# Second layer of a two-layer kernel: gating product one scan behind its block, residual's addition four turns later, picks' places in PSUM

## The chip, the cores and the metric

The kernel runs on one core of one Trainium2 chip. The time is that of one launch on the device, in microseconds (us). The kernel before takes 4823.72 us (median of three runs, 4823.07 to 4824.93).

## The reference, cut to what matters

Two layers run over 8192 tokens (four sequences of 2048) of width 256: `x + attention(norm(x))`, then `x + experts(norm(x))`, twice. The change touches the second layer alone: a selective scan (the "attention" of that layer), and the routing of the experts behind it.

```python
x_ssm, res = jnp.split(x @ W_in.T, 2, axis=-1)          # 512 channels each
x_ssm = silu(causal_conv4(x_ssm) + b_conv)
dt = softplus(x_ssm @ W_dt.T + b_dt)
# 16 states per channel: one recurrence over time for each of 512 x 16 pairs
h = exp(dt * A) * h + dt * B * x_ssm
y = h.sum(over states) + D * x_ssm
y = (y * silu(res)) @ W_out.T
x = x + y                                                # the residual
# two groups of 32 experts, the 2 best of each for every token
logits = norm(x) @ router_w;  expert_weights, expert_indices = top_k(softmax(logits), 2)
order = argsort(expert_indices)                          # every pick gets a row, sorted by expert
```

## The kernel before, in words

Engines: TensorE (PE), VectorE (DVE), ScalarE (ACT), GpSimd (POOL) and SyncE (SP, which issues most DMAs). Each has one queue of instructions and takes them strictly in the order in which the Python code emits them. Semaphores tie them together: `mark` counts an instruction, `after` makes the next instruction of an engine wait for marks.

The second layer works on 16 chunks of 512 tokens. The function `scans` is a loop over 64 recurrences ("scans") for each chunk: 4 blocks of 128 channels (`e`), with 16 states in each (`n`). In this text the scans of a chunk are numbered 0 to 63, so that block 0 ends with scan 15, block 1 with scan 31. In turn `g` of the loop are emitted, in this order:

- POOL: `dbx`, the input of two scans (L1528, every other turn); ACT: the decay exp(dt*A) of scan g into PSUM (L1535), which may be three scans ahead (`ND`).
- DVE: scan g-2 (L1546), into one of eight buffers `hs` (`NR`).
- DVE, after the last scan of a block: the gating product (L1553), which multiplies the finished sum of the block in PSUM bank 7 (`YB`) with silu(res), in turn g = last scan + 4. It waits for PE's sum of the block's last scan. One bank holds the sums of all blocks, so PE can't begin the next block's sum (L1567, the skip term; wait on `"y free"`) before this product has ended.
- PE: the sum over states, scan g-3: four 128x128 transposes that add into the bank (L1571). I call these four matmuls "a sum".
- `background.pull()`: pieces of other stages, at a fixed rate for each. The stage `after_scan` (rate 1.2 pieces a turn) takes the chunk before: four groups of transposes of the gated product (L1071), four of the product with `W_out` (L207, in two banks), a pause of `LAG + 2` pieces, the residual's addition (L1309, which waits for the product), norm statistics (L1036, L1040), the norm on ACT, transposes, the router, and the places of the picks (L1386 to L1394). The stage `main` (rate 0.8) prepares the chunk ahead: products with `W_in` (L207), a convolution by four matmuls with diagonal taps (L1164), silu on ACT with a table load on either side (L1173, L1174). `sizes` makes dt (L1232 to L1257). POOL scatters sorted rows by indirect DMAs (L1475).

These stages share four banks of PSUM (`G`). A stage that finds all four taken gives its turn back, so a bank that is held longer moves the other stages' instructions. The profile counts each fp32 matmul of the program twice where the moving side is 128x256 or 128x512 (two `W_in` matmuls are x4 in a row of the trace), and so for L1567; sums and transposes are counted once.

## Time and profile before

| | |
|---|---|
| median of three runs | 4823.72 us |
| profiled execution, its own time | 4822.83 us |
| its span, first to last instruction | 4821.0 us |
| first scan begins, last scan begins | 2502.5 us, 4142.5 us |
| scans that start in the second layer | 1024 (16 chunks of 64) |
| busy over the span | PE 89%, DVE 77%, POOL 62%, ACT 52% |
| busy in the scans' 200 us from 3200 us | PE 180.1, DVE 179.7, POOL 175.3, ACT 155.9 us |

Rows of the trace give the start (us from the span's first instruction), the time taken, the engine, the source line, the operation, what it writes and reads, and how many equal instructions the row merges. Brackets hold the idle time of that engine just ahead, and what ended it. An engine's instructions overlap a little: a scan of 1.25 us starts every 1.18 us.

### The profile page before, as it was taken

The numbers are of one execution on the slowest core, as the hardware profiler recorded it, in microseconds if no ns is written. First come the engines' busy times: TensorE is split into PE (matmuls) and PEld (weight loads), VectorE is DVE, ScalarE is ACT, GpSimd is POOL, SyncE is SP. The second block draws the span as 40 slices with busy tenths as digits, with TensorE's granted clock in tenths as the row PEclk, the third lists the DMA queues.
The fourth block names the chain that finished last, engine by engine and source line by source line (L and its number), as shares of the span: only waits on it lengthen the run. The fifth ranks groups of instructions, "written<-read, shape, count | busy, mean of one in ns | idle before, by whom it ended". The sixth has DMA issues, their size and how long they took to land. (4 is left out here: it accounts for less than half of the span.)

```text
span 4821.0 us, 59211 instructions
## 1 busy us (share of the span) xinstructions
PE 4269.6 (89%) x19350; PEld 2845.4 (59%) x19350; DVE 3709.2 (77%) x5917; ACT 2521.4 (52%) x4939; POOL 3002.8 (62%) x1908
## 2 busy tenths in 40 slices
PE   5689999999999999998989988989989988599993
PEld 1345566555566555565656566666556666488883
DVE  6887777787778787776128999988999989555677
ACT  1343334344334344333458777777877777255552
POOL 3445545465545455554147888888888889655552
PEclk7899999999999999999999999999999999699997
DMA  4233323333333333332121122121122122596887
GB/s 145 83 105 105 110 88 104 107 104 107 108 96 97 110 99 112 105 102 85 54 85 49 67 78 99 71 74 67 71 82 99 69 69 71 180 254 196 266 278 279
DMA packets 304193, 545.54 MB, mean 113 GB/s; under 512 B 31504, under 2 KB 148496, under 8 KB 294928
## 3 DMA queue, kind: packets, MB, share of 16 engines
q1 hardware_dynamic: 275664, 465.56, 30.0%
q0 software_dynamic: 27648, 75.67, 4.4%
q8 instruction: 157, 2.57, 0.2%
q14 instruction: 148, 1.21, 0.1%
q10 hardware_dynamic: 576, 0.53, 0.1%
HBM read 422.72 MB, written 118.92 MB: 112 GB/s over the span
## 5 line engine op out<-in xcount | busy, mean ns | idle before, releaser
L1528 POOL TENSOR_TENSOR c_dbx<-c_dtx,c_Brep 128x1024 f32<-128x1024 f32 x512 | 1203.0, 2363 | 159.2 <-DVE c_hs L1546 119.0
L876 POOL TENSOR_TENSOR a_kv<-a_rk,a_kv 128x512 f32<-128x512 f32 x512 | 807.3, 1589 | 404.4 <-DMA a_kv<-v_rows 404.2
L1546 DVE TENSOR_TENSOR_SCAN c_hs<-psum,c_carry,c_dbx 128x512 f32<-128x512 f32 x768 | 934.6, 1263 | 56.3 <-ACT psum L1535 41.7
L885 DVE TENSOR_TENSOR_SCAN a_S<-a_decay,a_carry,a_kv 128x513 f32<-128x513 f32 x512 | 792.6, 1548 | 181.6 <-POOL a_kv L876 93.3
L802 POOL TENSOR_TENSOR a_hid_e<-a_hid_e,a_g_rep 128x512 f32<-128x512 f32 x256 | 387.1, 1514 | 772.7 <-ACT a_hid_e L791 590.4
L1535 ACT ACTIVATE psum<-c_dt,c_cols 128x512 f32<-128x512 f32 x1024 | 695.2, 688 | 285.6 <-DVE c_hs L1546 283.6
L1571 PEld LDWEIGHTS psum<-ident,c_hs 128*128 128x128 f32 x4096 | 491.9, 145 | 343.2 <-DVE c_hs L1546 169.7
L1571 PE MATMUL psum<-ident,c_hs 128*128 128x128 f32 x4096 | 596.6, 282 | 87.3 <-DVE c_hs L1546 85.1
L891 DVE TENSOR_TENSOR a_prod<-a_rk,a_S 128x512 f32<-128x512 f32 x512 | 546.4, 1067 | 71.9 <-PE psum L907 71.8
L783 PE MATMUL psum<-a_W_down,a_hid_e 128*128 128x256 f32 x2304 | 550.8, 385 | 54.0 <-POOL a_hid_e L802 29.7
L207 PE MATMUL psum<-a_xT,a_W_up 128*128 128x512 f32 x1152 | 559.5, 616 | 14.7 <-ACT a_hid_e L791 14.6
L783 PEld LDWEIGHTS psum<-a_W_down,a_hid_e 128*128 128x128 f32 x2304 | 436.1, 192 | 219.3 <-issue 83.2
L1934 POOL DMA_INDIRECT results<-d_ys,d_to_row x320 | 312.1, 975 | 231.7 <-issue 154.4
L207 PEld LDWEIGHTS psum<-a_xT,a_W_up 128*128 128x128 f32 x1152 | 217.6, 194 | 253.3 <-issue 209.5
L791 ACT ACTIVATE a_hid_e<-psum 128x512 f32<-128x512 f32 x288 | 171.2, 595 | 339.6 <-PE psum L207 338.7
L2025 PE MATMUL psum<-d_w,d_xT 128*128 x1280 | 332.1, 382 | 0.9 <-issue 0.9
L1546 DVE TENSOR_TENSOR_SCAN c_hs<-psum,c_dbx 128x512 f32<-128x512 f32 x256 | 296.7, 1204 | 34.5 <-ACT psum L1535 18.3
L1475 POOL DMA_INDIRECT sorted_rows<-route_xn,route_to_row x240 | 245.5, 1023 | 84.1 <-issue 38.4
L1232 PE MATMUL psum<-c_xs,c_W_dt 128*128 128x512 f32 x512 | 269.5, 609 | 11.2 <-ACT c_gate L1195 11.2
L207 PE MATMUL psum<-a_xT,a_w 128*128 128x256 f32 x1024 | 239.9, 382 | 12.0 <-ACT a_decay L475 8.9
L658 PE MATMUL psum<-a_w,a_hid_f 128*128 128x256 f32 x1024 | 244.5, 382 | 6.0 <-DVE a_xb L674 3.4
L1164 PE MATMUL psum<-c_pre,c_taps 128*128 128x512 f32 x512 | 242.5, 596 | 0.0
(287 smaller groups left out, 6817.4 us busy)
## 6 DMA issues: line engine op xcount, KB each, us to landing
a_kv<-v_rows SPq DMA_DIRECT2D x512, 256.0 KB
a_g_rep<-g_rows SPq DMA_DIRECT2D x256, 256.0 KB, 3.9
c_Brep<-b_rows SPq DMA_DIRECT2D x64, 1024.0 KB, 6.0
d_xs<-sorted_rows SPq DMA_DIRECT2D x320, 128.5 KB
d_w<-results SPq DMA_DIRECT2D x64, 512.0 KB, 11.4
d_w<-in_d_experts SPq DMA_DIRECT2D x32, 768.0 KB
a_xa<-in_L_attn_x SPq DMA_DIRECT2D x16, 512.0 KB, 4.7
v_rows<-a_rv SPq DMA_DIRECT2D x16, 512.0 KB, 3.0
```

The costliest lines, as they stand in the source:

```text
L207: last = nc.tensor.matmul(out, lhsT, rhs, start=(n == 0), stop=(n == len(pairs) - 1))
L783: m_down = nc.tensor.matmul(banks[t // 2][1][:, (t % 2) * D:(t % 2 + 1) * D], hid_e[:, r, t * P:(t + 1) * P], W_down[:, q, :], start=(q == ...
L802: hid[e - 1] = m_done["gate used", n] = pool.mark(nc.gpsimd.tensor_tensor(hid_e[:, r, :], hid_e[:, r, :], g_rep[:, n % NG, :], ALU.mult))
L876: m_kv[g] = pool.mark(nc.gpsimd.tensor_tensor(kv[:, g % NV, 1:C + 1], rk[slot][:, 1, hb, :], kv[:, g % NV, 1:C + 1], ALU.mult))
L885: m_scan[q] = dve.mark(nc.vector.tensor_tensor_scan(S[:, q % NS, :], decay[cq % 2][:, hb, :], kv[:, q % NV, :], carry[:, sq_:sq_ + 1], ALU ...
L891: m_prod[q] = dve.mark(nc.vector.tensor_tensor(prod[:, q % NP, :], rk[cq % 2][:, 0, sq_ // DK, :], S[:, q % NS, 0:C], ALU.mult))
L1528: m_dbx[g] = m_dbx[g + 1] = pool.mark(nc.gpsimd.tensor_tensor(dbx[:, r:r + 2, :], dtx[slot][:, e, :].unsqueeze(1).broadcast_to([P, 2, C]), ...
L1535: m_da[g] = act.mark(nc.scalar.activation(psum[:, DA + g % ND, :], dt[slot][:, e, :], ACT.Exp, scale=A[:, e, n:n + 1]))
L1546: m_scan[q] = dve.mark(nc.vector.tensor_tensor_scan(hs[:, q % NR, :], psum[:, DA + q % ND, :], dbx[:, q % NX, :], first, ALU.mult, ALU.add))
L1571: last = nc.tensor.matmul(psum[:, YB, t * P:(t + 1) * P], hs[:, q % NR, t * P:(t + 1) * P], ident[:, :], is_transpose=True, start=False, s ...
L1934: nc.gpsimd.indirect_dma_start(out=results[j // NT], in_=ys[:, j % NY, :], in_offset=None, out_offset=bass.IndirectOffsetOnAxis(ap=to_row[ ...
L2025: m = nc.tensor.matmul(bank[:, 0:2 * P], xT[:, q % N3, kb * P:(kb + 1) * P], w[:, bass.ds(at_w[q] + kb * 2 * P, 2 * P)], start=(kb == 0), ...
```

## The change

Three edits, all in the second layer.

1. In `scans` the gating product is emitted behind PE's sum in turn g = last scan + 3, not ahead of it in turn g = last scan + 4.
2. The pause between the product with `W_out` and the residual's addition is `LAG + 6` pieces of the stage, not `LAG + 2`.
3. The places of the picks are reduced into the same PSUM bank as the ranks, not into an SBUF tile `place`; the bank is freed by the CAST that reads them, not by the product two instructions earlier.

```diff
-                yield from pause(LAG + 2)
+                yield from pause(LAG + 6)
...
-            ranks = bank[:, 0:TL * NE]
+            ranks, in_room = bank[:, 0:TL * NE], bank[:, TL * NE:TL * NE + TL * Z.picks]
...
-            m = G.freed[i] = dve.mark(nc.vector.tensor_tensor(
+            m = dve.mark(nc.vector.tensor_tensor(
                 at_pick[:, :, :, :], R["onehot"][:, :, :, :],
                 ranks.rearrange("p (r e) -> p r e", e=EX).unsqueeze(2).broadcast_to([P, TL * GR, TOP, EX]), ALU.mult))
...
-            m = dve.mark(nc.vector.tensor_reduce(flat(place[:, :, :, :].rearrange("p t g k -> p t (g k)")), at_pick[:, :, :, :].rearrange("p r s e -> p (r s) e"), AX, ALU.add))
+            m = dve.mark(nc.vector.tensor_reduce(in_room, at_pick[:, :, :, :].rearrange("p r s e -> p (r s) e"), AX, ALU.add))
...
-            m_done["placed", c] = [dve.mark(nc.vector.tensor_copy(flat(route.to_row[:, c % 2, :, :]), flat(place[:, :, :, :].rearrange("p t g k -> p t (g k)")))), m_xn]
+            m = G.freed[i] = dve.mark(nc.vector.tensor_copy(flat(route.to_row[:, c % 2, :, :]), in_room))
+            m_done["placed", c] = [m, m_xn]
...
-                q = g - AHEAD - 2
-                if 0 <= q < total and q % N == N - 1:
-                    cq, sq = divmod(q, steps)
-                    e = sq // N
-                    background.drain(until=lambda: is_done(("gate", cq)))
-                    dve.after(m_sum[q], m_done["gate", cq])
-                    m_done["gated", cq, e] = m_done["y free"] = dve.mark(nc.vector.tensor_tensor(
-                        gate[cq % 2][:, :, e * P:(e + 1) * P], psum[:, YB, :].rearrange("p (t d) -> p t d", t=TL),
-                        gate[cq % 2][:, :, e * P:(e + 1) * P], ALU.mult))
                 q = g - AHEAD - 1
...
                     if sq == steps - 1:
                         m_done["scanned", cq] = [m_dbx[q], m_da[q], m_sum[q]]
+                q = g - AHEAD - 1
+                if 0 <= q < total and q % N == N - 1:
+                    cq, sq = divmod(q, steps)
+                    e = sq // N
+                    background.drain(until=lambda: is_done(("gate", cq)))
+                    dve.after(m_sum[q], m_done["gate", cq])
+                    m_done["gated", cq, e] = m_done["y free"] = dve.mark(nc.vector.tensor_tensor(
+                        gate[cq % 2][:, :, e * P:(e + 1) * P], psum[:, YB, :].rearrange("p (t d) -> p t d", t=TL),
+                        gate[cq % 2][:, :, e * P:(e + 1) * P], ALU.mult))
```

The order of the program moves with it. Below, the eighth chunk (c = 7), whose pattern is that of chunks 1 to 14. Scans are named `SCALAR_TENSOR_TENSOR c_hs`.

DVE before, from behind scan 1 of the chunk to scan 17 and its neighbours (the L1553 rows are the gating products of the chunk before and of block 0):

```order
L1553 TENSOR_TENSOR c_gate<-psum,c_gate 128x4x128
L1254 TENSOR_TENSOR c_dtx<-psum,c_xs 128x512
L1546 SCALAR_TENSOR_TENSOR c_hs<-psum,c_carry,c_dbx 128x512 x14
L1309 TENSOR_TENSOR c_xb<-c_xb,psum 128x512 x2
L1546 SCALAR_TENSOR_TENSOR c_hs<-psum,c_carry,c_dbx 128x512
L1036 BN_STATS c_stats<-c_xb 128x6 x4
L1040 BN_AGGR c_mv<-c_stats 128x2 x4
L1546 SCALAR_TENSOR_TENSOR c_hs<-psum,c_carry,c_dbx 128x512
L1553 TENSOR_TENSOR c_gate<-psum,c_gate 128x4x128
```

The same stretch of DVE now (the gating product is L1574, scans are L1547):

```order
L1574 TENSOR_TENSOR c_gate<-psum,c_gate 128x4x128
L1250 SCALAR_TENSOR_TENSOR psum<-psum,c_tmp 128x512
L1547 SCALAR_TENSOR_TENSOR c_hs<-psum,c_carry,c_dbx 128x512
L1254 TENSOR_TENSOR c_dtx<-psum,c_xs 128x512
L1547 SCALAR_TENSOR_TENSOR c_hs<-psum,c_carry,c_dbx 128x512 x15
L1574 TENSOR_TENSOR c_gate<-psum,c_gate 128x4x128
L1309 TENSOR_TENSOR c_xb<-c_xb,psum 128x512 x2
L1547 SCALAR_TENSOR_TENSOR c_hs<-psum,c_carry,c_dbx 128x512
L1036 BN_STATS c_stats<-c_xb 128x6 x4
L1040 BN_AGGR c_mv<-c_stats 128x2 x4
```

Before, the addition stood behind scan 15 and the gating product of block 0 behind scan 17. Now the gating product stands behind scan 16, and the addition right behind it.

PE before, from the product with `W_out` to the sums of block 1 (each x4 of L1571 is one sum; the first L1567 row begins block 1):

```order
L1571 MATMUL psum<-ident,c_hs 128x128 x4
L207 MATMUL psum<-c_W_out,c_yT 128x256 x4
L1164 MATMUL psum<-c_pre,c_taps 128x512 x2
L1571 MATMUL psum<-ident,c_hs 128x128 x4
L207 MATMUL psum<-c_W_out,c_yT 128x256 x4
L1571 MATMUL psum<-ident,c_hs 128x128 x20
L207 MATMUL psum<-c_xT,c_W_in 128x512 x2
L1567 MATMUL psum<-c_skip_diag,c_xs 128x128 x4
L1571 MATMUL psum<-ident,c_hs 128x128 x4
L207 MATMUL psum<-c_xT,c_W_in 128x512 x2
L1571 MATMUL psum<-ident,c_hs 128x128 x20
L1164 MATMUL psum<-c_pre,c_taps 128x512 x2
```

PE now, from the last product with `W_out` (the sums are L1563, the skip term L1559):

```order
L207 MATMUL psum<-c_W_out,c_yT 128x256 x8
L1563 MATMUL psum<-ident,c_hs 128x128 x4
L1164 MATMUL psum<-c_pre,c_taps 128x512 x2
...
L1164 MATMUL psum<-c_pre,c_taps 128x512 x2
L1563 MATMUL psum<-ident,c_hs 128x128 x16
L1559 MATMUL psum<-c_skip_diag,c_xs 128x128 x4
L1563 MATMUL psum<-ident,c_hs 128x128 x12
L207 MATMUL psum<-c_xT,c_W_in 128x512 x2
L1563 MATMUL psum<-ident,c_hs 128x128 x4
L207 MATMUL psum<-c_xT,c_W_in 128x512 x2
L1563 MATMUL psum<-ident,c_hs 128x128 x20
L1164 MATMUL psum<-c_pre,c_taps 128x512 x2
```

The same pieces stand ahead of the sum of scan 15 as before, with the products ahead of the taps instead of among them. The two pairs of `W_in` that stood on either side of block 1's beginning now both come three and four sums into block 1. The first transposes of the gated product now stand ahead of the pair of `W_in` at the chunk's beginning, which before stood ahead of the wait for the gating product:

```order
L1563 MATMUL psum<-ident,c_hs 128x128 x24
L1071 MATMUL psum<-ident,c_gate 128x128 x4
L207 MATMUL psum<-c_xT,c_W_in 128x512 x2
L1559 MATMUL psum<-c_skip_diag,c_xs 128x128 x4
L1563 MATMUL psum<-ident,c_hs 128x128 x4
```

On ACT the silu of the second pair of blocks (L1173, with its two table loads) moves from turn 34 to turn 37 of a chunk.

## Rows read from the trace of the kernel before

**Rows 1.** Busy time of the engines in stretches: us, PE, PEld, DVE, ACT, POOL, clock, DMA.
```profile
3200.00:3400.00 200.00, 180.12 (x981) 121.36 (x979) 179.66 (x253) 155.86 (x282) 175.28 (x96) 0.98 0.20 71
...
3110.00:3112.00 2.00, 2.00 (x6) 0.96 (x4) 2.00 (x3) 1.69 (x4) 2.00 (x1) 0.50 0.00 0
```

**Rows 2.** Groups of DVE's instructions, 2510 to 4150 us: busy us, mean ns | idle before.
```profile
L1309 DVE TENSOR_TENSOR c_xb<-c_xb,psum 128x512 f32<-128x512 f32 x31 | 20.8, 675 | 68.5 <-PE psum L207 64.5 <-PE psum L1442 4.0
...
L1394 DVE CAST route_to_row<-c_place 128x16 int32<-128x16 f32 x15 | 11.1, 743 | 0.0
```

**Rows 3.** The line of the CAST, L1394: ns min/median/max.
```profile
L1394 DVE CAST route_to_row<-c_place x16: 139/199/2676, 2677.5 to 4185.6; 128x16 int32<-128x16 f32 x16
```

**Rows 4.** Timeline around one CAST, DVE and POOL.
```profile
3298.98 2.68 DVE L1394 CAST route_to_row<-c_place 128x16 int32<-128x16 f32 x1
3299.25 2.36 POOL L1528 TENSOR_TENSOR c_dbx<-c_dtx,c_Brep 128x1024 f32<-128x1024 f32 x1
```

**Rows 5.** The line of the gating product, L1553: DVE's idle before it; who waited.
```profile
  PE psum L1571: 0.8, 1
...
  PEld psum L1567: 116.6, 62
```

**Rows 6.** Timeline of DVE, chunk 7, scan 0 to the gating product of block 0.
```profile
3212.93 1.25 DVE L1546 TENSOR_TENSOR_SCAN c_hs<-psum,c_carry,c_dbx 128x512 f32<-128x512 f32 x1
...
3215.88 0.66 DVE L1553 TENSOR_TENSOR c_gate<-psum,c_gate 128x512 f32<-128x512 f32 x1
...
3217.06 11.84 DVE L1546 TENSOR_TENSOR_SCAN c_hs<-psum,c_carry,c_dbx 128x512 f32<-128x512 f32 x10
...
3235.24 0.66 DVE L1309 TENSOR_TENSOR c_xb<-c_xb,psum 128x512 f32<-128x512 f32 x1
3239.85 0.69 DVE L1309 TENSOR_TENSOR c_xb<-c_xb,psum 128x512 f32<-128x512 f32 x1 [3.95 <-PE psum L207]
3240.45 1.28 DVE L1546 TENSOR_TENSOR_SCAN c_hs<-psum,c_carry,c_dbx 128x512 f32<-128x512 f32 x1
3241.65 1.38 DVE L1036 BATCH_NORM_STATS2 c_stats<-c_xb 128x6 f32<-128x256 f32 x4
...
3243.47 1.25 DVE L1546 TENSOR_TENSOR_SCAN c_hs<-psum,c_carry,c_dbx 128x512 f32<-128x512 f32 x1
3244.64 0.66 DVE L1553 TENSOR_TENSOR c_gate<-psum,c_gate 128x512 f32<-128x512 f32 x1
```

**Rows 7.** Timeline of PE, the same stretch.
```profile
3213.56 1.88 PE L207 MATMUL psum<-c_xT,c_W_in 128*128 128x512 f32 x4
3216.60 1.16 PE L1567 MATMUL psum<-c_skip_diag,c_xs 128*128 128x128 f32 x8 [1.16 <-DVE c_gate L1553]
...
3235.77 1.88 PE L1164 MATMUL psum<-c_pre,c_taps 128*128 128x512 f32 x4
...
3237.92 1.89 PE L207 MATMUL psum<-c_W_out,c_yT 128*128 128x256 f32 x8
3239.65 2.35 PE L1571 MATMUL psum<-ident,c_hs 128*128 128x128 f32 x20
3241.83 1.88 PE L207 MATMUL psum<-c_xT,c_W_in 128*128 128x512 f32 x4
3245.36 1.16 PE L1567 MATMUL psum<-c_skip_diag,c_xs 128*128 128x128 f32 x8 [1.64 <-DVE c_gate L1553]
```

**Rows 8.** Timeline of DVE, the end of block 1 of that chunk.
```profile
3265.59 0.67 DVE L1553 TENSOR_TENSOR c_gate<-psum,c_gate 128x512 f32<-128x512 f32 x1
3268.03 1.28 DVE L1546 TENSOR_TENSOR_SCAN c_hs<-psum,c_carry,c_dbx 128x512 f32<-128x512 f32 x1 [1.78 <-ACT psum L1535]
```

**Rows 9.** Timeline of PE, the last two sums of that block.
```profile
3263.67 1.04 PE L1571 MATMUL psum<-ident,c_hs 128*128 128x128 f32 x8
```

**Rows 10.** Timeline of ACT, the silu of the second pair of blocks.
```profile
3263.24 1.28 ACT L1173 ACT_TABLE_LOAD   x1
...
3265.82 1.28 ACT L1174 ACT_TABLE_LOAD   x1
3267.12 0.30 ACT L1469 ACTIVATE route_xn<-route_xn,route_ones 128x4 f32<-128x4 f32 x1
```

More of the change, by code:

```diff
@@ L1601, in layer1_phase @@
         at_pick = sb("at_pick", [P, TL * GR, TOP, EX])
-        place, over = sb("place", [P, TL, GR, TOP]), sb("over", [P, NE])
+        over = sb("over", [P, NE])
         R = router_buffers(nc, st, "c", GR, EX, TOP)
```

## The prediction

> **What bounds the kernel now.** I read the busy time by stretches first. In the scans both PE and DVE are busy nine tenths of the time [rows 1], so shares alone name no bound; the question is who waits for whom at which scan. The groups of DVE's instructions come next: the largest wait of one small group is the residual's addition, 64.5 us in all for PE's product with W_out [rows 2], 14 waits, one in each of chunks 1 to 14. The line of the gating product shows the opposite: DVE has waited for PE only once there, 0.8 us, while PE's weight loads wait 116.6 us for the product [rows 5]. Both edits aim at these numbers. Last I read the timelines of DVE and PE side by side in chunk 7, where the clock was at its high level.
>
> What the reader is to see there: scan 15 ends at 3235.3, the addition begins, and its second half waits until 3239.85 [rows 6]. PE at that time is not slow at one product; it is seven us behind as a whole. From the skip term at 3216.60 to the sum of scan 15 it runs without a gap: five sums stand in one row behind the product, to 3242.0 [rows 7]. So the first quarter of a chunk is bound by PE: 25.4 us of matmuls against some 20 us of scans (16 at 1.18 us, from the row of ten [rows 6]). The rest of the chunk is mostly bound by DVE's own work.
>
> **Part 1, the addition and the gating product of block 0.** These two have one answer, since they now stand next to each other. The gating product needs the sum of scan 15, which is the last thing that PE does of its backlog, behind both products that the addition needs. When does that sum end now? The chunk's first gating product (block 3 of the chunk before) needs a sum behind which PE began the pair of W_in at 3213.56 [rows 7], before scan 0 ended, so it starts behind scan 0: 3212.93 + 1.18 = 3214.1 in place of 3215.88, 1.78 us earlier [rows 6]. But in front of it PE had the pair of W_in (from 3213.56, 1.88 us [rows 7]) as cover, and that pair now stands behind the first transposes, which wait for the product. PE starts at 3214.8 and has 25.4 + 1.7 us to do (the pair takes 1.72 until the next can start): 3241.9, against 3242.0 before. The early start is eaten by the lost cover; the rest is the same set of matmuls in another order. So the gating product starts at 3242.0 to 3242.1.
>
> DVE then: scan 16 now runs ahead of it (3235.2 to 3236.5), and DVE waits for 5.6 us, not 3.95. Behind the gating product come the two additions, scan 17, the statistics, and scan 18. By rows 6 the steps from start to start are 0.6 (product), 0.6 and 0.6 (additions), 1.2 (scan), 1.82 (statistics, 3241.65 to 3243.47): scan 18 starts at 3242.05 + 4.8 = 3246.9. Before, it started 0.58 us behind the product at 3244.64, so at 3245.2. DVE is 1.6 us later. The wait of the addition has not gone; it is the gating product's, and what DVE used to do between the end of W_out's product and the end of the sums (scan 16, statistics, scan 17) now stands behind them.
>
> **Part 2, block 1.** PE gets the bank 2.6 us earlier (3242.8 instead of 3245.36 [rows 7]) and would be glad of it, but has nothing to do: both pairs of W_in that stood here now come three and four sums later, and scans 17 and 18 end at 3245.1 and 3248.1. Before, PE went from 3245.36 to the end of sum 31 (3264.7 [rows 9]) in 19.35 us without a gap. Now it has one more pair of W_in in that stretch, 1.72, and I count 4.4 us of idle: 0.9 ahead of sum 17, 2.3 ahead of sum 18, and 1.1 ahead of sums 23 and 24, since the taps come at sum 25 and not at 22. 3242.8 + 19.35 + 1.72 + 4.4 = 3268.3, and the gating product of block 1 starts at 3268.4, not 3265.59 [rows 8]. It has scan 32 ahead of it but no longer scan 33. Scan 34 starts at 3268.4 + 0.6 + 1.2 = 3270.2; before at 3268.03, where it had waited 1.78 us for ACT [rows 8]. DVE is 2.2 us later (the 1.6 of part 1 are in it).
>
> ACT's block of silu and two table loads takes 3263.24 to 3267.12, 3.9 us [rows 10], and it caused that 1.78. It moves from turn 34 to turn 37, so the wait is not gone but comes again behind the gating product's. ACT is at most three scans ahead; with two small router instructions of DVE as cover I get a wait of 1.0 us at scan 37, and take 0.6 of it as new (bounds 0 and 1.78). Sum for a chunk: 2.8 us. Bounds: 1.6, if block 1 loses nothing of its own, and 4.5, if ACT's wait returns in full on top with another small one at the later silu. Times 14: +39 us, +22 to +63. In block 2, by the same timeline, PE's sum ends as scan 1 of the next block does, so the new place costs DVE nothing that counts; in block 3 it is early. Chunk 0, where PE still warms up, I put at +1. Chunk 15 has no W_in and no taps: 0.
>
> **Part 3, the places in PSUM.** One CAST of 128x16 took between 139 and 2676 ns [rows 3], 743 in the mean and 11.1 us for 15 [rows 2]. The long one ended within 0.05 us of POOL's product (3298.98 + 2.68 against 3299.25 + 2.36 [rows 4]): DVE stood still for the whole of POOL's instruction. With its input in PSUM I expect it to take 0.14 to 0.2 us, as the short ones do: (0.743 - 0.17) x 15 = -8.6 us, in block 3, where DVE is the bound. Bounds: -8.6 and 0 (it is held as before). I take -8. The bank is held two instructions longer, which moves some matmuls of W_dt by nothing and others by two sums, hidden in block 3, where PE waits.
>
> The Trainium skill explains this row ("SBUF — State Buffer", section "SBUF: two separate sides"): VectorE and GpSimd share a port pair as an exclusive lock, which a VectorE instruction takes in a two-port mode. By that rule the copy from PSUM needs no lock and the whole 8.6 goes; if the rule didn't hold for this CAST, the time would be 8 us more. The trace agrees with the lock, with its 2.68 us; that PSUM avoids it no run here shows yet.
>
> **Sum.** +39 + 1 - 8 = +32 us on the profiled execution's 4822.8 (its span is 4821.0), and the median of the runs lies 0.9 above that: 4855 us.
>
> **Rivals.** *A: the waits go, as the numbers of the profile suggest.* The addition's 64.5 us vanish and the 8 of the CAST too: 4823 - 64 - 8 = 4751; if half of it comes back elsewhere, 4783. For it: four more turns (3.3 scans, some 4 us) are just the mean wait, 64.5 / 14 = 4.6. Against it: DVE can't pass the gating product, and the sum that this needs ends at 3242, 2.2 us behind the product with W_out [rows 7]. It needs PE to finish the sum of scan 15 four us earlier than I reckon. The Trainium skill ("Perfetto Trace Analysis", section "Optimization Strategy") tells one to find the gaps of the busiest engine and make what they wait for come sooner; followed on the addition's row alone that gives this rival.
>
> *B: nothing to be told from no change* (within 0.2%, about 9.6 us, which is what a measurement of this kernel can tell). PE's 2.6 us earlier skip term carries through block 1, its idle time is filled, and DVE loses the 1.6 of part 1 alone: +22 - 8 - 5 = +9 or less, 4824 to 4832. For it: PE waits for the gating product in 62 of 64 blocks [rows 5]. Against: in the timeline PE has nothing to do at that place.
>
> *C: the loss is larger through PE's clock.* At 3110 to 3112 PE ran at 0.50 of its clock, its lower level of 1.2 GHz, and in these 2 us issued only 6 matmuls [rows 1]; this followed a stretch in which it had waited for scans. New idle of 4.4 us at the head of block 1, which is PE's critical stretch, may bring such a spell there: 3.4 us at half speed cost 1.7 in each of 14 chunks, with part 2's upper bound: 4823 + 63 + 24 - 8 = 4902. It decides only if idle comes in one piece, and mine comes in three.
>
> **How the numbers follow.** My forecast 0.66, its own range 4838 to 4878 (part 2's bounds and part 3's). A 0.12, B 0.14, C 0.08. The range 4808 to 4890 leaves out most of A and half of C. Faster by over 0.2%: A and a sliver of B, 0.14. Same: most of B and the low end of mine, 0.15. Slower: 0.71.
>
> **What would show it.** Right: L1309 no longer waits, and the gating product's line has some 14 waits for PE of 5 to 6 us (block 0) and 14 more of 1 to 3 us (block 1), over 85 us in all; PE's wait at the skip term falls from 116.6 [rows 5] to under 60, with new idle ahead of sums 17 and 18; the chunks' period grows by 2 to 4 us; the CAST's mean falls to below 200 ns. Wrong: if in block 0 the gating product waits for under 3 us, part 1 is wrong and A holds; if block 1's gating product doesn't wait, part 2 is; if the CAST still takes over 1 us at times, part 3.

## The result, and the profile after

The changed kernel takes 4900.36 us (median of 5 runs, 4898.63 to 4905.88), the kernel before 4824.93 beside it (5 runs, 4823.07 to 4831.39): ratio 1.0156, 95% interval 1.0142 to 1.0170, or 75 us more. The forecast was 4855, in a range of 4808 to 4890. The direction was right and the size was not. The profiled execution took 4900.36 us, its span 4898.6; its mean clock was 0.942, against 0.950 before. One slow execution, 13130 us in early_2_4 below, is left out of its ratio.

First the groups of DVE's instructions in the scans, 2510 to 4220 us (busy us, mean ns | idle before), which answer to [rows 2, 5]:

```profile
L1574 DVE TENSOR_TENSOR c_gate<-psum,c_gate 128x512 f32<-128x512 f32 x64 | 43.8, 685 | 127.6 <-PE psum L1563 127.0
...
L1309 DVE TENSOR_TENSOR c_xb<-c_xb,psum 128x512 f32<-128x512 f32 x30 | 19.1, 680 | 0.0
L1394 DVE CAST route_to_row<-psum 128x16 int32<-128x16 f32 x15 | 2.2, 148 | 0.0
```

The addition no longer waits (64.5 us before), and the CAST has become short. But the gating product, now L1574, waits 127 us for the sums (L1563), where it had waited 0.8. Its own line tells the other side (which engine sat idle for it: us, times):

```profile
  PE psum L1563: 127.0, 32
...
  PEld psum L1559: 29.1, 29
```

PE's wait at the skip term fell from 116.6 us [rows 5] to 29.1. So the wait changed hands: DVE now stands where PE stood. The timeline of DVE in chunk 7 (start us, us; scan 0 begins at 3245.2), to be laid beside [rows 6]:

```profile
3246.51 0.69 DVE L1574 TENSOR_TENSOR c_gate<-psum,c_gate 128x512 f32<-128x512 f32 x1
...
3255.61 10.68 DVE L1547 TENSOR_TENSOR_SCAN c_hs<-psum,c_carry,c_dbx 128x512 f32<-128x512 f32 x9 [2.50 <-ACT psum L1536]
...
3270.19 1.28 DVE L1547 TENSOR_TENSOR_SCAN c_hs<-psum,c_carry,c_dbx 128x512 f32<-128x512 f32 x1 [1.13 <-ACT c_carry L1555]
3276.87 0.69 DVE L1574 TENSOR_TENSOR c_gate<-psum,c_gate 128x512 f32<-128x512 f32 x1 [5.39 <-PE psum L1563]
3277.47 1.28 DVE L1309 TENSOR_TENSOR c_xb<-c_xb,psum 128x512 f32<-128x512 f32 x2
3278.66 1.28 DVE L1547 TENSOR_TENSOR_SCAN c_hs<-psum,c_carry,c_dbx 128x512 f32<-128x512 f32 x1
3279.86 1.38 DVE L1036 BATCH_NORM_STATS2 c_stats<-c_xb 128x6 f32<-128x256 f32 x4
...
3303.95 0.69 DVE L1574 TENSOR_TENSOR c_gate<-psum,c_gate 128x512 f32<-128x512 f32 x1 [2.71 <-PE psum L1563]
```

Block 0's product waits 5.39 us, and additions, scan 17 and statistics stand behind it, not in front. Block 1's waits 2.71. PE at the same time, beside [rows 7]:

```profile
3240.03 0.66 PE L1563 MATMUL psum<-ident,c_hs 128*128 128x128 f32 x4 [0.87 <-DVE c_hs L1547]
3241.80 0.95 PE L1563 MATMUL psum<-ident,c_hs 128*128 128x128 f32 x4 [1.12 <-DVE c_hs L1547]
3242.98 3.50 PE L1563 MATMUL psum<-ident,c_hs 128*128 128x128 f32 x12 [0.23 <-DVE c_hs L1547]
...
3248.23 3.62 PE L207 MATMUL psum<-c_xT,c_W_in 128*128 128x512 f32 x4
...
3274.92 1.91 PE L1563 MATMUL psum<-ident,c_hs 128*128 128x128 f32 x16
3277.61 1.16 PE L1559 MATMUL psum<-c_skip_diag,c_xs 128*128 128x128 f32 x8 [0.78 <-DVE c_gate L1574]
3278.61 0.60 PE L1563 MATMUL psum<-ident,c_hs 128*128 128x128 f32 x4
3280.00 0.66 PE L1563 MATMUL psum<-ident,c_hs 128*128 128x128 f32 x4 [0.79 <-DVE c_hs L1547]
3282.99 1.12 PE L1563 MATMUL psum<-ident,c_hs 128*128 128x128 f32 x4 [2.33 <-DVE c_hs L1547]
3283.89 3.13 PE L207 MATMUL psum<-c_xT,c_W_in 128*128 128x512 f32 x4
```

Two things are to be seen. Ahead of sums 17 and 18 PE is idle, as forecast. And a pair of W_in, 1.88 us in [rows 7], takes 3.62 us at the head of the chunk and 3.13 us behind that idle time. The windows of two of those stretches show why (us; busy of PE, PEld, DVE, ACT, POOL; granted clock; DMA):

```profile
3242.00:3246.00 4.00, 3.62 (x15) 2.42 (x14) 4.00 (x5) 3.97 (x8) 3.39 (x3) 0.50 0.74 279
3246.00:3249.00 3.00, 2.12 (x8) 1.32 (x7) 2.97 (x5) 1.35 (x4) 1.80 (x1) 0.50 0.00 0
```

The clock is 0.50, the lower level of 1.2 GHz, just where PE's backlog begins. Added up over the scans, PE ran at that level for 133 us before and for some 210 us after. At the heads of the chunks it did so in 7 of 15 before and in 11 of 15 after, in block 1 in 1 of 14 and in 12 of 14. From the first scan's start to the last's it is 1640.0 us before and 1709.0 after, so 69 of the 75 us lie in the scans.

For the comparisons below I took from each trace the start of every scan, subtracted that of its chunk's scan 0, averaged over chunks 2 to 13 and subtracted the same of before. It is the delay (us) that a chunk has gathered by then; at "64" the next chunk begins. Where two kernels have different work of DVE ahead of a scan, the difference there is not lost or gained time; only the last row is free of that. The kernels are explained below.

```
scan  early_12  late_12  gate_only  pause_only   after  keep_all  psum_keep
 18     +0.5     +1.9      +0.3       -2.3       +2.9     +1.6      -0.1
 34     +0.4     +1.2      +0.7       +0.1       +4.4     +2.1      -0.2
 38     +0.4     +1.2      +2.1       -0.5       +5.5     +3.2      -0.2
 48     +0.4     +1.9      +3.7       -0.9       +6.1     +3.8      -0.2
 52     -0.2     +1.2      +5.1       -1.6       +5.4     +3.1      -0.9
 54     -0.2     +0.1      +5.1       +4.5       +4.3     +2.0      -0.9
 64     -0.2     +1.2      +5.1       +4.5       +5.4     +3.1      -0.9
scan   early_4  early_1_4  early_2_4  early_3_4  early_4_keep
 18     -1.3      -0.3       -1.6       -1.2        -2.7
 34     -2.2      -1.7       -0.6       -2.2        -3.6
 38     -2.1      -1.5       +0.7       -2.0        -3.4
 48     -1.0      -0.2       +2.6       -0.8        -2.2
 64     -1.4      -0.4       +2.6       -0.5        -2.3
```

### The profile page after: what moved, and what is told of

The parts are those of the page before. It is cut to its first block and busy times, and to the rows that moved or that the text cites. A ratio compares the mean times of both kernels' runs of the same rounds, so it can differ in the third digit from the quotient of the medians.

```text
span 4898.6 us, 59190 instructions
## 1 busy us (share of the span) xinstructions
PE 4312.5 (88%) x19350; PEld 2860.5 (58%) x19350; DVE 3705.2 (76%) x5917; ACT 2515.2 (51%) x4939; POOL 2998.6 (61%) x1908
## 5 line engine op out<-in xcount | busy, mean ns | idle before, releaser
L1547 DVE TENSOR_TENSOR_SCAN c_hs<-psum,c_carry,c_dbx 128x512 f32<-128x512 f32 x768 | 938.7, 1268 | 65.4 <-ACT psum L1536 52.8
L1563 PEld LDWEIGHTS psum<-ident,c_hs 128*128 128x128 f32 x4096 | 503.0, 147 | 411.0 <-DVE c_hs L1547 217.3
L1563 PE MATMUL psum<-ident,c_hs 128*128 128x128 f32 x4096 | 622.4, 287 | 119.8 <-DVE c_hs L1547 117.2
L1547 DVE TENSOR_TENSOR_SCAN c_hs<-psum,c_dbx 128x512 f32<-128x512 f32 x256 | 297.3, 1208 | 38.4 <-ACT psum L1536 22.9
```

The costliest lines, as they stand in the source:

```text
L1547: m_scan[q] = dve.mark(nc.vector.tensor_tensor_scan(hs[:, q % NR, :], psum[:, DA + q % ND, :], dbx[:, q % NX, :], first, ALU.mult, ALU.add))
L1563: last = nc.tensor.matmul(psum[:, YB, t * P:(t + 1) * P], hs[:, q % NR, t * P:(t + 1) * P], ident[:, :], is_transpose=True, start=False, s ...
```

## Experiments: each edit alone

The kernel before was measured again beside each group of runs, and its medians lie between 4813.85 and 4824.93 us. So ratios are compared, not times. An expectation given as a time is to be read against 4824.9: 4890 us, for instance, is the ratio 1.0135. In the traces, what lies outside the scans varies from 3170 to 3190 us in no order that follows the edits; the starts of the scans are free of it.

**gate_only.** The kernel before with the product's block moved behind the sum, `q = g - AHEAD - 2` becoming `q = g - AHEAD - 1` (the hunks at 1544 and 1573 of the change).

> The kernel before with the first edit alone: the gating product one scan behind its block; the addition's pause and the picks' places as before. Theory 1 (order and clock): this edit alone moves the matmuls of W_in and the taps, so block 1 suffers as in the changed kernel, but the addition now stands behind scan 13, and the product with W_out comes two sums earlier on PE, so L1309 hardly waits (under 10 us in all against 64.5) and the additions, the statistics and their scan are done before the gating product of block 0, which waits only 2 to 4 us. Scan 18 of a chunk starts about 3 us earlier than in the changed kernel. Expected: 4825 to 4850 us, 50 to 75 below the changed kernel. Rival 2 (the gating edit carries the whole loss, the pause nothing): 4890 to 4909.

Measured: 4882.84 us, ratio 1.0144 (1.0128 to 1.0159). My theory missed, and the number is that of rival 2: this edit alone brings nearly the whole loss. And it doesn't arise in blocks 0 and 1, as I had it, but between scans 34 and 50. There, ACT's silu of the gates with its table loads now stands at turn 48, and the product of block 2 right behind it. Scan 48 waits for ACT 28.1 us in 14 chunks, and the product then 27.0 us for PE (DVE, chunk 7):

```profile
3330.22 1.28 DVE L1546 TENSOR_TENSOR_SCAN c_hs<-psum,c_carry,c_dbx 128x512 f32<-128x512 f32 x1 [1.56 <-ACT psum L1535]
3332.38 0.69 DVE L1573 TENSOR_TENSOR c_gate<-psum,c_gate 128x512 f32<-128x512 f32 x1 [0.87 <-PE psum L1562]
```

**pause_only.**

```diff
-                yield from pause(LAG + 2)
+                yield from pause(LAG + 6)
```

> The kernel before with the second edit alone: pause of LAG + 6. Theory 1: the gating product of block 0 (still two scans behind) now stands ahead of the addition and waits some 4 us for PE's sum, in place of the addition's 4.6; W_in keeps its place, so PE loses nothing and gets the bank 1.7 to 2.6 us earlier. Expected 4805 to 4830. Rival 2 (the pause is what hurts): over 4860. Rival 3 (the addition's wait simply goes, 64 us): 4760 to 4775.

Measured: 4877.04 us, ratio 1.0138 (1.0123 to 1.0154). Missed as well; the number is that of rival 2, and it arises in one place. DVE waits for the rank matmuls (PE's rows, then DVE's, chunk 7):

```profile
3324.34 2.08 PE L1567 MATMUL psum<-c_skip_diag,c_xs 128*128 128x128 f32 x8 [3.77 <-DVE c_gate L1553]
...
3333.22 0.70 PE L1354 MATMUL psum<-route_picked,route_ones 128*128 128x256 f32 x2
```

```profile
3333.96 0.70 DVE L1360 TENSOR_REDUCE route_picked<-route_picked 128x64 f32<-128x320 f32 x1 [4.35 <-PE psum L1354]
```

The pause moves everything behind it in its stage. The rank matmuls went from turn 47 to 51, past the skip term of block 3, which waits for the gating product. DVE waited 53.9 us in 13 such places. In the changed kernel they stand at 48, ahead of the skip term, and this wait isn't there. The -1.6 at scan 52 in the table is no lead: the two reductions, the product and the CAST that before stand behind scans 48 to 50 here come behind scans 53 and 54, and up to scan 52 DVE has been idle 0.7 us per chunk more than before.

**psum_only** (the third edit alone: `in_room = bank[:, TL * NE:...]` as output of the reduce and input of the copy, `G.freed` behind the copy).

> The kernel before with the third edit alone: the picks' places in PSUM. No instruction changes its place. Theory: the CAST's mean falls from 743 to about 150 ns and the time by 8 to 9 us: 4815 to 4818. Rival: the gain is taken up by a wait for POOL just behind, since POOL is free only then: 4822 to 4826.

Measured: 4810.47 us, ratio 0.9991 (0.9982 to 1.0000), some 4 us of the 8 to 9 expected. The CAST took 149 to 174 ns, as expected. In the trace this kernel gains 0.8 us per chunk, 11 us in 14 (10 us from the first scan to the last), a little more than the times allow (0 to 9 us).

The single edits give 1.0144, 1.0138 and 0.9991, all three together 1.0156: the losses don't add up, since most of the second edit's is a place that the first clears.

## Experiments: the clock

**keep_busy** is the changed kernel with matmuls of zeros that add nothing to the sum, at sums behind which PE waits for a scan at the end of a chunk:

```diff
                     m_sum[q] = pe.mark(last)
+                    if e == EB - 1 and 10 <= n < N - 1:
+                        for t in range(2):
+                            nc.tensor.matmul(psum[:, YB, t * P:(t + 1) * P], nothing[:, :], ident[:, :], start=False, stop=False, skip_group_check=True)
```

> The changed kernel with two more matmuls of zeros added into the bank of the sums after each of the sums 58 to 62 of a chunk, where PE only waits for scans; they change no value. Theory 1: about 1.3 us of each chunk's loss is PE's lower clock (0.5) at the head of the chunk, behind PE's idle end of block 3. With PE busy there, the sum of scan 15 ends 29.0 to 29.3 us behind scan 0 in all chunks (mean before the change 29.1, changed 30.4), and the time falls by 15 to 25 us: 4875 to 4885. If the clock stays low or the theory is wrong: 4898 to 4905, or more, since the zeros cost PE some time.

Measured: 4868.49 us, ratio 1.0107 (1.0092 to 1.0123), at the favourable end of what the clock theory said (1.0104 to 1.0125 as ratios). By the ratios half a per cent, 24 us, comes back from doing more work; from the first scan to the last the traces have 14 us less.

**keep_all** adds 4, 12, 6 and 5 more behind sums 16, 17, 34 and 38.

> The changed kernel, with matmuls of zeros added into the sums' bank wherever PE waits for scans: 2 after each of sums 58 to 62, and new 4 after sum 16, 12 after sum 17, 6 after sum 34, 5 after sum 38. In the changed kernel PE ran at 0.50 of its clock for 210 us within the scans; with only the first group of these matmuls it was 122 us, the spells at the head of the chunks were gone, those at 34 to 41 us in a chunk stayed, and the ratio to before fell from 1.0156 to 1.0107. Theory (half of the loss is the clock, half the order of the work): the spells in block 1 go too, low clock under 60 us, sum 31 ends 26.5 us after sum 15 and not 27.4, another 0.8 us per chunk come back: ratio 1.006 to 1.010. Rival (the clock in block 1 costs nothing, since DVE and ACT wait there for each other anyway): ratio stays at 1.011. If the added matmuls are themselves in the way: 1.012 or more.

Measured: 4862.87 us, ratio 1.0082 (1.0068 to 1.0096), low clock 36 us in the scans. The theory held: by the ratios the changed kernel's low clock is worth 36 us, from the first scan to the last 29. The head of a chunk (PE, chunk 7), then DVE at the end of block 0:

```profile
3230.79 0.61 PE L1567 MATMUL psum<-ident,c_nothing 128*128 128x128 f32 x4
3231.50 0.66 PE L1563 MATMUL psum<-ident,c_hs 128*128 128x128 f32 x4
3233.35 0.63 PE L1071 MATMUL psum<-ident,c_gate 128*128 128x128 f32 x4 [1.19 <-DVE c_gate L1576]
3233.81 1.88 PE L207 MATMUL psum<-c_xT,c_W_in 128*128 128x512 f32 x4
```

```profile
3260.45 0.69 DVE L1576 TENSOR_TENSOR c_gate<-psum,c_gate 128x512 f32<-128x512 f32 x1 [4.31 <-PE psum L1563]
3261.06 1.28 DVE L1309 TENSOR_TENSOR c_xb<-c_xb,psum 128x512 f32<-128x512 f32 x2
```

The pair of W_in is back at 1.88 us. In this kernel the sum of scan 15 ends 29.05 us after scan 0 starts in the mean, in the changed one 30.37.

**psum_keep** is psum_only with such matmuls (2 behind sums 58 to 62, 3 behind 44 and 45): does the low clock cost anything before the change?

> The kernel before with the places in PSUM (alone it had the ratio 0.9991) and with matmuls of zeros: 2 after each of sums 58 to 62, 3 after sums 44 and 45. Before, PE ran at 0.50 for 133 us within the scans, mostly at scans 48 to 53, where PE waits anyway, and at the head of five chunks. Theory: only the spells at the head of a chunk cost, some 0.5 us per chunk in the mean, so a ratio of 0.997 to 0.999, the best so far. Rival: the low clock costs before as much as after (about 2 us per chunk): 0.993. Rival: the added matmuls cost what they gain: 1.000 or more.

Measured: 4810.84 us against 4824.29 for before, ratio 0.9973 (0.9964 to 0.9983). As expected, little: 0.2% beside psum_only, with low clock down to 75 us, from 133 before and 119 in psum_only.

## Experiments: the join and the order

Moving the products does two things. It moves the places at which DVE must wait for PE (the join). And since `after_scan` begins when block 3's product is emitted, it moves the other work (W_in from turns 1, 16, 17, 32, 34 to 4, 19, 20, 35, 36; silu from 34 and 45 to 37 and 48; the addition from 16 to 14 without the longer pause). These kernels take the places per block, all with the third edit:

```diff
+                if ... q % N == N - 1 and q % steps // N in LATE:    # q = g - AHEAD - 2, ahead of the sum
...
+                if ... q % N == N - 1 and q % steps // N in EARLY:   # q = g - AHEAD - 1, behind the sum
```

**early_12**: blocks 0 and 1 early, `pause(LAG + 2)`.

> The kernel before with the places in PSUM, and only the gating products of blocks 0 and 1 one scan behind instead of two; those of blocks 2 and 3, and the order of all other work (products, taps, silu, addition at turn 16) stand as before. This is the join of DVE and PE moved, without the order. Theory: block 0 costs the 1.6 us of part 1, block 1 up to 1 us more, since PE gets the bank early but finds no scans: 1.6 to 2.6 us in 14 chunks, less 4 for the places: ratio 1.004 to 1.007, the product waits some 5 to 6 us at scan 16. Rival (it is the order of the matmuls that costs, the join is free): ratio 0.999 to 1.001. Rival (all of the loss is the join): 1.012 to 1.016.

Measured: 4821.88 us, ratio 0.9993 (0.9984 to 1.0002), beside 0.9991 for psum_only. In the old order the early joins are free within the noise, as the first rival had it and my theory did not; from the first scan to the last it takes 6 us more than psum_only. DVE, chunk 7:

```profile
3239.09 0.69 DVE L1309 TENSOR_TENSOR c_xb<-c_xb,psum 128x512 f32<-128x512 f32 x1 [3.97 <-PE psum L207]
3239.69 1.28 DVE L1547 TENSOR_TENSOR_SCAN c_hs<-psum,c_carry,c_dbx 128x512 f32<-128x512 f32 x1
3241.27 0.69 DVE L1583 TENSOR_TENSOR c_gate<-psum,c_gate 128x512 f32<-128x512 f32 x1 [0.30 <-PE psum L1572]
```

The addition's wait of 4 us stands in front of the product; PE finishes its backlog under it, and the product finds its sum ready but for 0.30 us.

**late_12**: the changed kernel with blocks 0 and 1 late (2 and 3 early, `pause(LAG + 6)`).

> The changed kernel in all but one thing: the gating products of blocks 0 and 1 stand two scans behind as before; the order of all other work is that of the changed kernel. This is the order without the join. Theory (both cost, and the clock follows from the idle at the head of block 1): ratio 1.004 to 1.009, with fewer spells of low clock at 34 to 41 us of a chunk. Rival (all of the loss is the join): ratio 0.999 to 1.001. Rival (all of it is the order): 1.014 to 1.016.

Measured: 4835.67 us against 4824.29, ratio 1.0024 (1.0015 to 1.0034). That is between the first rival and the theory's range. So taking the two joins back recovers 1.3 of the 1.56%, though alone they cost nothing that can be told.

**early_4**: only block 3 early, `pause(LAG + 2)`.

> The kernel before with the places in PSUM, and only the gating product of block 3 one scan behind: this starts the work behind the scans earlier and so gives the order of the first edit alone (W_in at turns 4, 19, 20, 35, 36 for 1, 16, 17, 32, 34; silu at 37 and 48 for 34 and 45; addition at 14), while the products of blocks 0, 1 and 2 stay two scans behind. The first edit alone had 1.0144, and lost 4.7 us of its 5.1 per chunk between scans 36 and 50. Theory (the loss there needs both, the later silu and the join at the end of block 2): ratio 1.003 to 1.008. Rival (the order alone): 1.012 to 1.015. Rival (the joins alone): 0.998 to 1.001.

Measured: 4794.98 us against 4816.0, ratio 0.9958 (0.9944 to 0.9972). All three theories missed: the new order alone is a gain. PE, then DVE, at the end of block 0 in chunk 7:

```profile
3234.84 1.91 PE L1572 MATMUL psum<-ident,c_hs 128*128 128x128 f32 x16
3237.53 1.16 PE L1568 MATMUL psum<-c_skip_diag,c_xs 128*128 128x128 f32 x8 [0.78 <-DVE c_gate L1554]
3238.53 1.47 PE L1572 MATMUL psum<-ident,c_hs 128*128 128x128 f32 x12
3239.84 1.88 PE L207 MATMUL psum<-c_xT,c_W_in 128*128 128x512 f32 x4
```

```profile
3226.13 1.26 DVE L1309 TENSOR_TENSOR c_xb<-c_xb,psum 128x512 f32<-128x512 f32 x2
...
3236.79 0.69 DVE L1554 TENSOR_TENSOR c_gate<-psum,c_gate 128x512 f32<-128x512 f32 x1 [2.74 <-PE psum L1572]
```

The addition doesn't wait, and the late products of blocks 0 and 1 now wait too (53.1 us in 26 places in all). DVE does scans 16 and 17 before the product, so three sums (x12) follow the skip term without a gap: the idle time of PE ahead of sums 17 and 18 needs the product in front of those scans.

**early_1_4, early_2_4, early_3_4**: block 3 and one other block early: block 0, 1 or 2 (the labels count blocks from 1).

> As the kernel with only block 3's product one scan behind (ratio 0.9958), and block 0's too. By the traces the first edit alone (all four products early, 1.0144) falls back by 1.6 us per chunk at scan 18, by 1.4 more at scan 34, by 1.2 at scan 38 and by 2.0 at scan 50. Theory (each join costs its own piece, block 0's the 1.6 us of part 1): 1.6 x 14 = 22 us over 0.9958: ratio 0.999 to 1.002. Rival (block 0's join pulls the whole loss behind it, since DVE, ACT and PE then stay in step): 1.010 or more. Rival (block 0's is free, as it was in the old order): 0.996.

> As the kernel with only block 3's product one scan behind (0.9958), and block 1's too. Theory (its own piece, 1.4 us at scan 34, and the wait for ACT's silu at scan 37, 1.1 us, since DVE has no scan left to run ahead with): 1.4 to 2.6 us in 14 chunks, ratio 1.000 to 1.004. Rival (free): 0.996. Rival (without block 0's join it costs only the wait at scan 34): 0.999.

> As the kernel with only block 3's product one scan behind (0.9958), and block 2's too. In this order ACT's silu of the gates (with two table loads) stands at turn 48, and DVE waits for it at scan 48, 1.5 us in 14 chunks, with the product of block 2 behind. Theory (the product then waits for PE as well, as in the first edit alone, where it waited 2.4 us): 1 to 2 us in 14 chunks, ratio 0.999 to 1.002. Rival (free: PE is in front there once blocks 0 and 1 have no early join): 0.996.

Measured: 0.9985 (0.9977 to 0.9994), 1.0056 (1.0043 to 1.0069) and 0.9987 (0.9978 to 0.9996). Beside early_4's 0.9958 the early product costs 0.3% in block 0, 1.0% in block 1 and 0.3% in block 2. The first and the third lie just beneath the theory, the second above it. The three sum up to 1.5%, and gate_only (which lacks the third edit) is 1.9% above early_4. So each join costs its own piece in this order; block 1's is dearest. In gate_only the loss seemed to arise behind scan 34 alone because up to there the new order's gain (early_4: -2.2 at scan 34) covers most of what the joins of blocks 0 and 1 cost (gate_only: +0.7). The early products in early_2_4 (which they waited for: us, times; 15 of the 16 are block 1's):

```profile
  PE psum L1572: 45.5, 16
```

By the table early_2_4 is 1.6 us behind early_4 at scan 34, 2.8 at scan 38 (DVE now waits 1.2 us for ACT's silu at scan 37 in each of 14 chunks, and in early_4 not at all), 3.6 at scan 48 and 4.0 at the end.

late_12 and early_3_4 differ in the pause alone: blocks 2 and 3 early in both, `LAG + 6` in the first and `LAG + 2` in the second. Their ratios are 1.0024 and 0.9987, so the second edit costs 0.37% in this order too. I had made no expectation for this pair.

**act_before and act_after**: psum_keep and keep_all with the silu of the second pair of blocks as an identity and its two table loads left out, in chunks 2 to 15.

```diff
-                    ... activation(xs_[:, e, :], bank, ACT.Silu, bias=b_conv[:, e, :]))
-                nc.scalar.preload_act_table_set("natural_log_exp_and_others")
+                    ... activation(xs_[:, e, :], bank, ACT.Identity if e0 and c > 1 else ACT.Silu, bias=b_conv[:, e, :]))
+                if not (e0 and c > 1):
+                    nc.scalar.preload_act_table_set("natural_log_exp_and_others")
```

> The same left out (silu of the second pair and its two table loads in chunks 2 to 15) in the kernel before with the places in PSUM and the matmuls of zeros (ratio 0.9973). There DVE waits for ACT 1.6 us at scan 34 and 1.4 at scan 31. Theory (ACT's block costs before 1.6 per chunk, as much as or more than after, so that ACT explains little of the difference): ratio 0.990 to 0.994. Rival (the wait at scan 34 is cover for PE and nothing is gained): 0.997. If ACT is what the change made worse, this gains clearly less than the same edit does in the changed kernel.

> The changed kernel with all the matmuls of zeros (ratio 1.0082, low clock 36 us), and left out: the silu of the second pair of blocks in chunks 2 to 15 is an identity, without its two table loads (2 x 1.28 us of ACT per chunk). There DVE waited for ACT 15.1 us in 14 at scan 37, 8.8 us at scan 42, 14.0 us at scan 32. Theory (the waits of 1.03 at scan 37 come from this block and count in full, those at scan 42 belong to the gates' silu and stay, the one at scan 32 hides behind PE): 1.0 us per chunk less, 14 us: ratio 1.004 to 1.006. Rival (the wait turns into one for PE): 1.007 to 1.008. Rival (ACT sets the pace of the whole block): 1.003 or less.

Measured: act_before 0.9913 (0.9899 to 0.9926), from 0.9973; act_after 1.0043 (1.0029 to 1.0057), from 1.0082. By the starts of the scans it is 1.9 us per chunk before and 1.2 after, both near what was expected (1.6 and 1.0). The wait for ACT costs in both, and no more after than before.

**pk_p4**: psum_keep with `pause(LAG + 4)`.

> The kernel before with the places in PSUM and the matmuls of zeros (ratio 0.9973), and the pause ahead of the addition two turns longer: the addition stands at turn 18, behind the gating product of block 0, and not at 16; all gating products stay two scans behind. The pause of four turns alone lost 1.4% by one place only: the rank matmuls came behind the skip term of block 3, and DVE waited 4.35 us for them; up to scan 52 that kernel was 1.6 us per chunk ahead of before. Here they stand at turn 48, ahead of the skip term. Theory: the loss is gone and about 1 us per chunk of the gain stays: ratio 0.993 to 0.997. Rival (the addition's wait only moves to the gating product, 5 us at scan 17, and nothing is gained): 0.997 to 0.999. Rival (any shift of the router's chain loses as in the single edit): over 1.005.

Measured: 4832.8 us against 4816.0, ratio 1.0035 (1.0021 to 1.0049): between the rivals, and a loss. The theory rested on a lead of pause_only up to scan 52, which was none, as said there. The gating product waited 66.2 us in 14 places, and DVE waited for ACT 30.1 us in 14 at scan 34 and 16.7 in 10 at scan 39. Why ACT comes late there I have not settled.

**early_4_keep**: early_4 with the matmuls of keep_busy.

> The kernel with only block 3's product one scan behind (0.9958) with matmuls of zeros, 2 after each of sums 58 to 62. In it PE ran at 0.50 for 58 us around the heads of the chunks, and scan 5 came 1.62 us later after scan 0 than before, with a wait for PE of 22.3 us in 14. Theory (the clock at the head costs what it shows there): that wait goes and about 1 us per chunk comes back, the best version: ratio 0.992 to 0.994. Rival (DVE catches up later anyway, the added matmuls gain as little as in the old order, 0.2%): 0.994 to 0.996.

Measured: 4768.11 us against 4813.85, ratio 0.9899 (0.9885 to 0.9914). It is the fastest version, 46 us below before, and by the ratio gains more than expected (0.6% over early_4, 28 us; from the first scan to the last, 15 us). The pair of W_in at the head of chunk 7 takes 1.88 us, in early_4 3.04. DVE is 1.4 us further ahead at scan 18 than in early_4, and 0.9 at scan 64.

## Why the prediction was wrong in size

Two terms of the sum failed. PE's clock stood at nothing in it, and the runs put it at 2.3 us per chunk, some 32 us. And part 2 took 0.6 us for ACT's waits behind scan 34, which are 1.7 us per chunk, some 15 us more. The mechanism of parts 1 and 2, a wait that changes hands, was right.

**Part 1 (block 0) was right without the clock.** It said that the sum of scan 15 ends 29.0 us after scan 0 starts, as before, and DVE is 1.6 us later at scan 18. In keep_all these are 29.05 and +1.6. In the changed kernel they are 30.37 and +2.9: the difference, 1.3 us per chunk, is the low clock at the head, of which the text said nothing for this place. The product waits 5.39 us in chunk 7 (5.6 forecast).

**Part 2 (block 1) was right as far as scan 34 and too small behind it.** It said +2.2 at scan 34; keep_all has +2.1. The product of block 1 waits 38.5 us in 16 blocks (1 to 3 us each forecast). Behind scan 34 I stopped counting, at 2.8 per chunk. Measured without the clock it is keep_all against psum_keep, 3.1 + 0.9 = 4.0 us, within part 2's bounds. The term that was mis-sized is ACT's wait. In keep_all DVE waits for ACT at scan 37 (1.1 us per chunk, 15.1 us in 14) and again at scan 42 (8.8 us in 14), and in psum_keep at neither (chunk 7, scans 37 and 42):

```profile
3294.09 1.28 DVE L1547 TENSOR_TENSOR_SCAN c_hs<-psum,c_carry,c_dbx 128x512 f32<-128x512 f32 x1 [1.03 <-ACT psum L1536]
...
3303.52 1.28 DVE L1547 TENSOR_TENSOR_SCAN c_hs<-psum,c_carry,c_dbx 128x512 f32<-128x512 f32 x1 [0.57 <-ACT psum L1536]
```

The wait at scan 37 was forecast (1.0), but only 0.6 of it was taken as new; the one at scan 42 stood in the upper bound alone, and it stays in act_after (8.8 us), so it isn't the second pair's silu. Nor is ACT what the change made worse as a whole: that silu costs 1.9 us per chunk before and 1.2 after, and without it the two kernels are further apart, 1.9 + 2.8 = 4.7 us per chunk. My reading is that behind an early join DVE has no scan in hand and meets each late partner separately. early_2_4 against early_4 fits it, with its wait at scan 37, but no run isolates it.

**Rival C was the mechanism that was missing, and it had 0.08.** After minus keep_all is 5.4 - 3.1 = 2.3 us per chunk, 32 us, and by the ratios 0.74% or 36 us. C put 1.7 us per chunk on block 1 and said that it decides only if idle comes in one piece. Ahead of the pair of W_in in block 1 it came in pieces of 0.78, 0.79 and 2.33 us in the rows above, and the pair took 3.13 us. More than half of the cost (1.3 of 2.3 us by scan 18) arose at the head of the chunk, where PE waits 0.2 to 1.1 us for each of the last scans before the backlog starts. Before, such spells stood at the head as well, in some chunks; [rows 1] shows one, and its pair of W_in took 3.54 us where [rows 7] has 1.88:

```profile
3109.57 0.74 PE L1571 MATMUL psum<-ident,c_hs 128*128 128x128 f32 x4 [0.52 <-DVE c_hs L1546]
3110.10 3.54 PE L207 MATMUL psum<-c_xT,c_W_in 128*128 128x512 f32 x4
```

I should have asked what more of them would cost.

**Part 3 was right on the CAST, and its time is within what was measured**: 148 ns in the mean; 8 us taken, 4 measured (0 to 9). With its input in PSUM the longest CAST is 174 ns, where it had been 2676 [rows 3]. The Trainium skill ("SBUF — State Buffer", section "SBUF: two separate sides") describes the lock on the ports that VectorE and GpSimd share; the trace agrees with it.

**Rival A** is refuted: the 64.5 us of the addition went, and 127 us stand at the gating product. **Rival B** needed PE's idle time filled, and it was not.

**The sum.** Per chunk +4.0 (the first two edits without the clock) + 2.3 (clock) - 0.9 (places, and what the added matmuls gain before) = +5.4, times 14 = 75 us. These are means of chunks 2 to 13; the periods of chunks 1 to 14 give +5.0, or 70 us, and the agreement with 75 is partly luck. Forecast: 2.8 x 14 + 1 - 8 = 32 (with 4822.8 and the 0.9 that makes 4855.7, put down as 4855).

**What I had not asked.** I took the change as one thing. Its first edit holds a gain (block 3's product early, -0.33% beside psum_only, which starts the work behind the scans sooner) and three losses (blocks 0 to 2). The second edit is a loss by itself: the longer pause cost 1.4% alone, 0.37% in late_12 against early_3_4, and 0.6% in pk_p4 against psum_keep. In pause_only and pk_p4 the addition no longer waits, and the time still grows. In late_12 PE ran at 0.50 for 123 us at the heads of the chunks, in early_3_4 for 91, which may be part of its cost; the rest stays open.

## What to carry to other kernels

A wait of a busy engine is worth taking away only if the engine it waits for isn't behind as a whole: ask when that engine's backlog ends, and what else joins it before then. Where the place of an instruction also starts other work, split the two: here the same move was good in the one block that starts the next stage, and in that new order bad in the three that only join two engines. And look at the clock at the head of each stretch in which the matmul engine is the bound; a few matmuls of zeros into a bank that is being summed anyway test in one run whether it costs. A scan that starts sooner is no gain while work that used to stand ahead of it stands behind: compare whole periods, or the engine's idle time.

## What the runs showed of the hardware

- With PE waiting 0.2 to 1.1 us for each scan ahead of a backlog, the backlog began at 0.50 of the clock in 11 of 15 chunks, and in chunk 7 a pair of W_in took 3.62 us for 1.88. Two zero matmuls (0.61 us) behind five sums per chunk removed these spells at the head (82 us in all after, 0 in keep_busy) and gave back 0.5% of the kernel's time by the ratios, 0.3% by the starts of the scans; in early_4, 0.6% and 0.3%.
- Not every such stretch ends in a spell: before, 7 of 15 heads had one, and chunk 7, with five such waits of 0.52 to 1.12 us, had none.
- Before the change the low clock cost less: psum_keep took 44 us of it away from psum_only's 119, 24 of these at the heads, and gained 0.2%.
